# Shared FFN down matmuls in three float32r terms, with split weights and slices

## The reference, cut to what matters

```python
x = x + xattn(layernorm(x), ctx, ...)      # x: 4 x 1024 x 256, ctx: 4 x 77 x 256
# xattn: h = tanh(txt_proj[b,t] + feat_proj[b,f] + bias); rho = h . w; softmax over the 77 rows;
#        the weighted text gives a gate w_s and a shift b_s per token: w_s * x + b_s
# then the FFN on layernorm(x):
probs = softmax(x @ gate)                  # 8 experts
scores, token_idx = top_k(probs.T, k=512)  # each expert takes its 512 best tokens of 4096
h = gelu(tok @ W1 + b1); out_tok = h @ W2 + b2          # 256 -> 1024 -> 256, per expert
routed = scatter_add(out_tok * scores)
shared = gelu(x @ Ws1 + bs1) @ Ws2 + bs2   # 4096 tokens x 256 -> 1024 -> 256
x = x + routed + shared
```

## Time and profile before

| what | us |
| --- | --- |
| median of three runs (898.47 to 903.25) | 899.86 |
| the profiled execution | 903.03 |
| its span, first to last instruction | 901.3 |
| mean granted TensorE clock, share of full speed | 0.982 |
| tanh of block 0 begins / of block 156 begins | 22.0 / 619.1 |
| first up matmul of an expert begins | 696.0 |

### The profile page before, as it was taken

How to read it: one execution, slowest core, us unless ns; L and a number is a source line. 1 busy time by engine, 2 the same in 40 slices (tenths; PEclk the granted TensorE clock), 3 DMA queues, 4 the chain that set the end, 5 groups by cost and what they waited for, 6 DMA issues and landing times.

```text
span 901.3 us, 14092 instructions
## 1 busy us (share of the span) xinstructions
PE 802.9 (89%) x5355; PEld 471.8 (52%) x5355; DVE 710.3 (79%) x1412; ACT 767.6 (85%) x600; POOL 314.0 (35%) x563
## 2 busy tenths in 40 slices
PE   6875579669997999999999999999889999999995
PEld 4321113114442444445354455545766999999985
DVE  4799889897989689988879995884887877667640
ACT  2999999999999999999999999997752676766771
POOL 3310640525444007774002740061303145554423
PEclk8899999999999999999999999999999999999998
DMA  8000000000001000200000010003102365554512
GB/s 263 19 1 1 1 1 1 1 24 1 24 1 47 1 1 1 94 1 1 24 1 1 24 48 1 24 1 117 48 24 77 106 170 140 141 127 108 137 20 34
DMA packets 32405, 41.80 MB, mean 46 GB/s; under 512 B 2365, under 2 KB 29011, under 8 KB 32339
## 3 DMA queue, kind: packets, MB, share of 16 engines
q1 hardware_dynamic: 26083, 32.49, 10.8%
q0 software_dynamic: 6144, 8.39, 5.6%
q10 hardware_dynamic: 112, 0.04, 0.0%
HBM read 28.33 MB, written 12.58 MB: 45 GB/s over the span
## 4 chain that ended last, share of the span: by engine, by line
PE 42%; ACT 37%; issue 10%; DVE 8%; POOL 2%; DMA 1%; ACTq 0%; DVEq 0%; POOLq 0%
ACT z L971 31%; PE bank L890 10%; PE bank L913 9%; PE bank L770 8%; PE bank L821 5%; DVE z L1329 3%; PE bank L806 3%; ACT z L967 2%; ACT u L1008 2%; PE bank L746 1%; PE bank L699 1%; PE bank L928 1%; PE bank L864 1%; DMA vec_rows<-in_L_xattn_w_dram 1%; ACT L1008 1%
## 5 line engine op out<-in xcount | busy, mean ns | idle before, releaser
L971 ACT ACTIVATE z<-z 128x4096 f32<-128x4096 f32 (+5 forms) x157 | 520.7, 3362 | 6.8 <-DVE z L1329 6.6
L1329 DVE TENSOR_SCALAR z<-feat,txt_bias 128x1024 f32<-128x1024 f32 (+1 forms) x722 | 421.2, 657 | 34.8 <-PE bank L770 33.6
L770 PE MATMUL bank<-z,window 128*32 128x512 f32 x2464 | 307.3, 609 | 62.9 <-ACT z L971 61.4
L770 PEld LDWEIGHTS bank<-z,window 128*32 128x32 f32 x2464 | 70.3, 110 | 252.5 <-issue 136.8
L821 PE MATMUL bank<-ws_sb,u 128*128 128x256 f32 x512 | 128.2, 391 | 5.5 <-ACT u L1008 5.5
L821 PEld LDWEIGHTS bank<-ws_sb,u 128*128 128x128 f32 x512 | 93.3, 192 | 41.5 <-issue 19.8
L806 PE MATMUL bank<-tr,ws_s 128*128 128x512 f32 x384 | 107.5, 416 | 0.0
L890 PE MATMUL bank<-xg_s,w_s 128*128 128x512 f32 x384 | 99.6, 397 | 0.2 <-DVE xg_s L1631 0.2
L913 PEld LDWEIGHTS bank<-w_s,hid_s 128*128 128x128 f32 x672 | 86.4, 188 | 4.0
L913 PE MATMUL bank<-w_s,hid_s 128*128 128x256 f32 x672 | 88.2, 280 | 0.0
L1044 ACT ACTIVATE hid<-bank,vec 128x512 f32<-128x512 f32 x64 | 44.2, 690 | 49.4 <-PE bank L890 49.3
(11 more groups left out here) (237 smaller groups left out, 785.6 us busy)
## 6 DMA issues: line engine op xcount, KB each, us to landing
...
x_ring<-in_x_dram SPq DMA_DIRECT2D x8, 512.0 KB, 7.9
xn_dram<-xn SPq DMA_DIRECT2D x8, 512.0 KB, 2.9
out_dram<-x_ring SPq DMA_DIRECT2D x8, 512.0 KB, 2.9
...
xg<-xn_dram,idx POOLq DMA_INDIRECT x32, 3.6
out_dram<-y,idx POOLq DMA_INDIRECT x32, 3.8
```

What stands on the lines that cost most here:

```text
L770: ins = e.matmul(sums[v][32 * r:32 * r + 32, :], window[:, c, 31 - k:63 - k], z[:, n % ZB, at_piece:at_piece + TOK], start=(v, r) not in b ...
L971: e.activation(part, part, ACT.Tanh).then_inc(signal(*step), 1)
L1329: ins = e.tensor_scalar(z[:, n % ZB, i * width:(i + 1) * width], feat_of(units, c), bias_of(units, t, c), None, ALU.add)
```

## The change

The down matmuls take both factors as rounded part and rest, in float32r, and add up three products: rest x part, part x rest, part x part (SPLIT_TERMS). For this

- Ws2 is split at the start in four steps `split_ws2` (part and rest for each half) on GpSimd, at slots 10, 12, 14 and 16 of batch 0; the raw weights are loaded into the u ring's space.
- each gelu slice gets `u_hi`, a rounding copy, on VectorE (for units 0 to 5; `u_hi_last` on GpSimd for 6 and 7), and `u_lo`, slice minus part, on GpSimd. The ring u holds both, so it is twice as large. Gelu writes where the rest goes later.
- FFN_PLACES grows to five stages: up one slot before, gelu one after, u_hi two, u_lo three, down six after (before: up, gelu, down at -1, 1, 2). FFN and the TAIL and PRE places move, and so do the fills behind the loop. Unit 7's downs stand two slices behind its ups instead of one. Of unit 5, the down steps of slices 5, 6 and 7 now come behind the loop (before: slice 7).
- SBUF is laid out anew: one xn2 buffer instead of two, tables of the start and of the router over others' space. This brings waits: `y_norm` of a unit waits for the turn and the store of the unit before; `values` waits for an early tanh; `pick` is cleared by GpSimd behind the loop (`pick_clear`) and no longer at the start. Expert 1 no longer waits for the stored outputs of units 6 and 7 before it rounds its w2.

```diff
@@ -33,30 +33,30 @@
-FFN_STEPS = ("up", "gelu", "down", "down_end", "store_out", "load_x")
+FFN_STEPS = ("up", "gelu", "u_hi", "u_lo", "down", "down_end", "store_out", "load_x")
...
-PRE_EARLY = (17, 19, 20, 22, 23, 23, 27, 24, 28, 29, 30)
-PRE_LATE = (25, 27, 28, 31, 32, 32, 34, 34, 36, 35, 39)
-TAIL_EARLY = (0, 0, 1, 4, 5, 5, 5, 4, 11, 6, 10, 12, 12, 14)
-TAIL_FIRST = (0, 0, 1, 3, 3, 4, 6, 6, 9, 6, 11, 11, 11, 13)
-TAIL_LATE = (0, 1, 2, 3, 8, 9, 10, 9, 13, 11, 15, 16, 16, 24)
-TAIL_SINGLE = (-1, 0, 1, 2, 3, 5, 5, 9, 12, 10, 11, 10, 11, 13)
...
-FFN_PLACES = (-1, 1, 2)
-FFN = ((8, 2.2), (34, 2.1), (13, 2.3), (36, 2.0), (13, 1.5), (26, 1.6))
+PRE_EARLY = (17, 19, 21, 22, 23, 24, 26, 25, 29, 30, 31)
+PRE_LATE = (22, 27, 28, 31, 32, 32, 32, 34, 35, 35, 39)
+TAIL_EARLY = (0, -1, 1, 3, 4, 4, 4, 3, 11, 6, 10, 11, 12, 15)
+TAIL_FIRST = (0, 0, 1, 3, 4, 4, 6, 6, 9, 6, 10, 11, 11, 13)
+TAIL_LATE = (0, 1, 2, 3, 8, 10, 10, 9, 15, 14, 17, 18, 19, 25)
+TAIL_SINGLE = (0, 0, 1, 2, 3, 5, 5, 8, 10, 10, 11, 10, 11, 12)
...
+FFN_PLACES = (-1, 1, 2, 3, 6)
+FFN = ((8, 2.1), (36, 2.0), (13, 3.1), (36, 2.0), (13, 1.8), (26, 1.6))
...
-TAIL_FILL = (8, 4)
-GELUS_BEFORE = 1
+TAIL_FILL = (5, 5)
+GELUS_BEFORE, RESTS_BEFORE = 1, 2
...
-TEST_FILL = (4, 4, 6, 5, 2, 5, 5, 5, 2, 1)
-RANK_FILL = (4, 3, 4, 4)
-EXPERT_FILL = (20, 6, 0)
-SECOND_FILL = (9, 2, 1, 5, 11)
-LIST_FILL = (2, 2, 0, 0)
+TEST_FILL = (1, 5, 4, 4, 4, 6, 4, 5, 4, 1)
+RANK_FILL = (4, 3, 4, 3)
+EXPERT_FILL = (24, 8, 3)
+SECOND_FILL = (7, 2, 1, 4, 8)
+LIST_FILL = (3, 2, 1, 0)
...
@@ -154,6 +154,7 @@
+    at_slots(0, (10, 12, 14, 16), [[("split_ws2", i, h)] for h in range(2) for i in range(2)])
...
@@ -174,7 +175,7 @@
-            at_slots(n, FFN_PLACES, [[("up", v, m, 0, passes)], [("gelu", v, m)], [("down", v, m, 0, J)]])
+            at_slots(n, FFN_PLACES, [[("up", v, m, 0, passes)], [("gelu", v, m)], [("u_hi", v, m)], [("u_lo", v, m)], [("down", v, m, 0, J)]])
...
@@ -204,11 +205,17 @@
     def fill(n=1):
...
-            if filler:
-                order.extend(filler.pop(0))
+            for step in filler.pop(0) if filler else []:
+                order.append(step)
+                if step[0] == "gelu":
+                    order.extend((("u_hi_last", *step[1:]), ("u_lo", *step[1:])))
     def up(v, m):
...
+    def rounding(steps):
...
+        return [(name, *step[1:]) for step in steps if step[0] == "gelu" for name in ("u_hi_last", "u_lo")]
...
@@ -219,7 +226,8 @@
-    last_ffn = up(vb, 0) + [piece for m in range(1, M) for piece in up(vb, m) + down(vb, m - 1)] + down(vb, M - 1)
+    last_ffn = up(vb, 0) + up(vb, 1) + [piece for m in range(2, M) for piece in up(vb, m) + down(vb, m - 2)]
+    last_ffn += down(vb, M - 2) + down(vb, M - 1)
...
@@ -239,14 +247,18 @@
+    order += [step for step in lead if step[0] in ("u_hi", "u_lo") and step[1:3] not in late]
+    waiting = {step[1:3] for step in lead if step[0] in ("u_hi", "u_lo")}
+    late |= waiting
...
+    rests = rounding(held)
...
-    order += [*end[7], *end[9], *end[8], ("logits_exp", vb), ("router", vb), ("values", NT - 2 * J, NT)]
+    order += [*end[7], *rests[:2 * RESTS_BEFORE], *end[9], *rests[2 * RESTS_BEFORE:], *end[8], ("logits_exp", vb), ("router", vb), ("values", NT - 2 * J, NT)]
...
@@ -254,7 +266,7 @@
-    order.append(("digits",))
+    order += [("digits",), ("pick_clear",)]
...
@@ -262,11 +274,11 @@
-        order += [("count", k), ("sign_count", k), ("total", k), *held, *(by_scalar.pop(0) if by_scalar else [])]
+        order += [("count", k), ("sign_count", k), ("total", k), *held, *rounding(held), *(by_scalar.pop(0) if by_scalar else [])]
...
-    order += held
+    order += [*held, *rounding(held)]
...
@@ -449,38 +456,43 @@
-        picked = sb("picked", [P, P], F32R)
...
-        pick = sb("pick", [P, NT, 32], BF16)
-        vals = sb("vals", [P, NT, E, V], BF16)
-        iota_slot = gt[:, 0:P]
-        rest = scan[:, 1, :].rearrange("p (t e) -> p t e", e=E)
-        b2_raw = eq[0:B2_ROWS, :]
...
+        feat_at = cursor[0]
...
-        xn2 = sb("xn2", [P, 2, J, D])
+        xn2 = sb("xn2", [P, J, D])
...
+        att_at = cursor[0]
...
+        b2_raw = sb("b2_raw", [B2_ROWS, D], at=att_at)[:]
+        iota_slot = sb("iota_slot", [P, P], at=att_at + 4 * D)[:]
+        vec_rows = sb("vec_rows", [NV, P], at=att_at + 4 * (D + P))
+        assert D + 2 * P <= 2 * J * R
+        tmp_at = cursor[0]
...
+        ws_sb = sb("ws_sb", [P, C, D], at=tmp_at)
+        assert C * D <= 2 * J * R
...
-        ws_sb = sb("ws_sb", [P, C, D])
+        cursor[0] = max(cursor[0], feat_at + 8 * C * WIDTH + 4 * (2 * HC * TOK + 2 * A * D))
...
-        ws2_sb = sb("ws2_sb", [P, M, D])
+        ws2_s = sb("ws2_s", [P, 2, M, D], F32R)
...
-        u = sb("u", [P, UR, TOK])
+        u_at = cursor[0]
+        u = sb("u", [P, UR, 2, TOK], F32R)
+        u_in = sb("u_in", [P, UR, 2, TOK], at=u_at)
...
@@ -493,7 +505,21 @@
+        tested = sb("tested", [P, NH * P])
+        eq = sb("eq", [P, NH * P])
+        gt = sb("gt", [P, NH * P])
+        picked = sb("picked", [P, P], F32R)
+        assert cursor[0] <= feat_at
+        cursor[0] = feat_at
...
+        vals = sb("vals", [P, NT, E, V], BF16)
+        rest = sb("rest", [P, NT, E])
+        scan = sb("scan", [P, 2, NH * P])
+        pick = sb("pick", [P, NT, 32], BF16)
+        assert cursor[0] <= feat_at + 4 * C * WIDTH and B % 2 == 0
+        cursor[0] = feat_at + 4 * C * WIDTH
...
+        assert cursor[0] <= feat_at + 8 * C * WIDTH
...
@@ -514,7 +540,10 @@
-        ws1_raw = u[:, 0:C * H // TOK, :].rearrange("p m s -> p (m s)").rearrange("p (c h) -> p c h", c=C)
+        u_flat = u_in[:].rearrange("p m i s -> p (m i s)")
+        ws1_raw = u_flat[:, 0:C * H].rearrange("p (c h) -> p c h", c=C)
+        ws2_raw = u_flat[:, C * H:C * H + M * D].rearrange("p (m d) -> p m d", m=M)
+        assert C * H + M * D <= 2 * UR * TOK
...
@@ -637,7 +667,7 @@
-            e.dma_start(ws2_sb[:], Ws2.rearrange("(m p) d -> p m d", p=P)).then_inc(loaded["ws2"], 16)
+            e.dma_start(ws2_raw, Ws2.rearrange("(m p) d -> p m d", p=P)).then_inc(loaded["ws2"], 16)
...
@@ -651,7 +681,7 @@
-                                xn2[:, v % 2]).then_inc(xn2_stored[v], 16)
+                                xn2[:]).then_inc(xn2_stored[v], 16)
...
@@ -809,17 +839,19 @@
                 elif kind == "down":
...
-                        e.wait_ge(loaded["ws2"], 16)
+                        for h in range(2):
+                            e.wait_ge(*done("split_ws2", 1, h))
...
-                    e.wait_ge(*done("gelu", v, m))
+                    e.wait_ge(*done("u_lo", v, m))
...
-                        ins = e.matmul(banks[DOWN[j // 2]][:, j % 2 * D:(j % 2 + 1) * D], u[:, m % UR, j * P:(j + 1) * P],
-                                       ws2_sb[:, m, :], start=False, stop=m == M - 1, skip_group_check=True)
+                        for term, (i, k) in enumerate(SPLIT_TERMS):
+                            ins = e.matmul(banks[DOWN[j // 2]][:, j % 2 * D:(j % 2 + 1) * D], u[:, m % UR, i, j * P:(j + 1) * P],
+                                           ws2_s[:, k, m, :], start=False, stop=m == M - 1 and term == 2, skip_group_check=True)
...
@@ -1005,7 +1037,10 @@
-                    e.activation(u[:, m % UR], banks[up_bank(v, m)][:], ACT.Gelu_apprx_tanh,
+                        for h in range(2):
+                            e.wait_ge(*done("split_ws2", 1, h))
...
+                    e.activation(u_in[:, m % UR, 1], banks[up_bank(v, m)][:], ACT.Gelu_apprx_tanh,
...
@@ -1020,8 +1055,6 @@
-                        e.wait_ge(stored[va], 16)
-                        e.wait_ge(stored[vb], 16)
...
@@ -1177,16 +1209,40 @@
                 elif kind == "y_norm":
...
-                    if v > 1:
-                        e.wait_ge(*done("y_turn", v - 2, C - 1))
-                        e.wait_ge(xn2_stored[v - 2], 16)
-                    normalise(x_ring[:, v % XB], xn2[:, v % 2], x_mv[:, v, :, 0], y_ry[:, v % 2]).then_inc(signal(*step), 1)
+                    if v > 0:
+                        e.wait_ge(*done("y_turn", v - 1, 0))
+                        e.wait_ge(*done("y_turn", v - 1, C - 1))
+                        e.wait_ge(xn2_stored[v - 1], 16)
+                    normalise(x_ring[:, v % XB], xn2, x_mv[:, v, :, 0], y_ry[:, v % 2]).then_inc(signal(*step), 1)
                 elif kind == "whole":
...
+                elif kind == "pick_clear":
+                    e.wait_ge(*done("tanh", LAST - 1))
+                    e.memset(pick[:], 0.0).then_inc(signal(*step), 1)
+                elif kind == "split_ws2":
+                    i, h = args
+                    part = slice(h * M // 2, (h + 1) * M // 2)
+                    e.wait_ge(loaded["ws2"], 16)
+                    if i == 0:
+                        e.tensor_copy(ws2_s[:, 0, part], ws2_raw[:, part]).then_inc(signal(*step), 1)
+                    else:
+                        e.wait_ge(*done("split_ws2", 0, h))
```

(18 more changed lines are left out.)

13 lines of the change are left out of this document (4 added, 9 removed).

## The result

The changed kernel takes **947.9 us** (median of four, 947.3 to 949.6) against 899.8: 1.053 times, 95% interval 1.051 to 1.055. It is slower, as forecast, but the forecast was +12 us and it is +48. The profiled execution took 949.58 us, its span is 947.8.

What follows compares the result with a forecast made beforehand. ScalarE was taken to bound the tanh loop, with the router's search and TensorE's experts behind it. Start +6, loop +8 and behind the loop -2 gave +12 us, 912 us against the median; range 896 to 928.

Steps and rivals of the forecast that it cites:

- start +6: At the start, four split_ws2 operations on GpSimd delay VectorE, for which ScalarE waits: +6 us, between 0.6 and 9.
- loop +8: In the tanh loop, u_hi and u_lo exceed VectorE's idle time in some units, so ScalarE waits: +8 us, limits 0 and 48.
- behind the loop -2: Behind the loop, shorter downs and better filled tests against added slices and waits: -2 us, from -6 to +4.
- A slice's cost in the loop: In the loop, each slice costs VectorE 0.41 us for u_hi and 0.9 for u_lo's port hold, 1.3 us together.
- Two more slices ... +2.8: Behind the last rho, unit 5's slices 5 and 6 now stand there too: +2.8 us.
- GpSimd's fill-time operations don't hurt the counts much; VectorE is there on short steps: Behind the loop, GpSimd's operations during the fill were said to hurt the counts little, VectorE being on short steps.
- The +2.6 at gather 0: Unit 7's slices 6 and 7: rounding queues on GpSimd behind gather 0, their downs ahead of the gathered rows' first turn: +2.6 us.
- The layout, nothing: The single xn2 buffer, moved tables, stores and later clears each counted as nothing; up to 3 us if a load is late.
- (a): Rival: the port is cheap; loop 0, start +1, tail -2 to -5, giving 896 to 899 us; chance 0.22.
- (b): Rival: TensorE's saving counts, in the stretch from 619 to 697 us, giving 892 us; chance 0.13.
- (c): Rival: in the loop, u_lo late in GpSimd's queue blocks TensorE, 2 to 3 us in five units, giving 925; chance 0.15.
- (d): Rival: in the tests, less fill lowers TensorE's clock, +1.7 us each time, inside the tail's range; no chance of its own.

Runs made afterwards that it cites:

- run 1: The changed kernel's order and layout with the old arithmetic (float32 downs, no split_ws2, u_hi, u_hi_last or u_lo), against the kernel before: 915.3 us, ratio 1.017.
- experiment 3: The kernel of run 1 without the line putting unit 5's last down behind unit 6's eight half-ups: 909.5 us; the same edit in the changed kernel: 945.6 us.
- small rounding: The changed kernel with all 64 u_lo and 16 u_hi_last over 4 columns a partition, downs reading the rounded slice in all three terms: 917.3 us.
- run 4: The changed kernel with the u_lo of units 0 to 5 over 4 columns instead of 512, downs reading the rounded slice in all three terms: 929.4 us.
- the holds alone: The kernel of run 1 plus 16 GpSimd casts and 16 subtractions into scratch beside the slices of units 6 and 7, no down waiting: 925.9 us.

## Why the prediction was wrong

The forecast was +12 us, in three terms: start +6, loop +8, behind the loop -2. Two of its steps failed. Behind the loop it took GpSimd's new steps and the rewritten order as nearly free (-2, measured +22.7); this is the larger miss. In the loop it took all of VectorE's idle time in the stretches of the slices as usable (+8, measured +18.8). In medians, each step against the one above it:

| kernel | us | step |
|---|---|---|
| before | 899.9 | |
| + new layout | 903.1 | +3.1 |
| + new order, float32 downs | 915.3 | +12.3 |
| + three terms, u_hi, split_ws2, small u_lo | 917.3 | +2.0 |
| + rounding of units 6 and 7 | 929.4 | +12.1 |
| + u_lo in the loop | 947.9 | +18.5 |

- **The start, +6: right.** The tanh of block 20 comes 5.7 us later behind the first tanh than in run 1, and 7.2 later than in the kernel before. The terms were right too: subtractions of 2.36 and 2.60 us for an estimated 2.9, casts of 1.16 and 1.51 for 1.6 to 2.2.
- **A slice's cost in the loop: right and a little high.** u_hi 0.47 us on average (0.42 median) for 0.41, u_lo 1.46 median for 1.5, its cost to VectorE 0.8 us for 0.9 (the adds' sum on the page went from 421.2 to 465.0 us; 4.9 of that is the start's). VectorE was busy 52.6 us longer where 63 were forecast.
- **The loop's sum, +8: the mechanism right, the size wrong.** The step that failed is "its idle time is spare capacity": summed by unit, all of VectorE's idle time in the six stretches (55.8 us) was counted as usable. Over the whole loop, of 72.8 us 33.8 were used. Of the 39.0 left, 15.8 are still waits for a free z buffer, so at other moments than those where time is short, and some 14 are waits for turns, statistics and gates. And u_hi brings idle time of its own (5.9 us), since it waits in the queue for its GELU. So the loop grew by 18.8, and not by 8; 2 to 4 of that are TensorE's wait for u_lo. The new order, taken as nothing in the loop, adds 1 to 3.
- **Behind the loop, -2: wrong, at +22.7** (274.2 to 296.9), in these terms. (i) "Two more slices ... +2.8" counted their matmuls and not who stands behind them: down_end of unit 5 waits at the head of VectorE's queue, ahead of the last `weigh`. Run 1 reaches the turn of the probabilities 9.0 us later behind the last tanh than the kernel before; 5.5 of them go with the one line of experiment 3, and the other 3.5 were not taken apart. (ii) "GpSimd's fill-time operations don't hurt the counts much; VectorE is there on short steps" was true of the counts (0.47 us in both) and wrong by 12.1 us of what it left out: the steps between two counts and those of the ranks (0.49 us became 1.58, 1.22 became 1.97). Tests and ranks are one serial chain in which each wait counts, and that a step is short did not help it. (iii) The saving of 5.4 us on downs was worth 2.5 (284.3 against 286.8 us behind the last tanh, small rounding against run 1). (iv) The -2.5 of the tests' new fill was right, in run 1: 25.2 us against 27.5. With the rounding they take 29.7. The -1 of the ranks did not come. (v) The +2.6 at gather 0 came (14.4 us from the first expert's gather to the second's for 12.1), but only in part by the rounding: run 1, without any, has 14.1, three terms with small rounding 12.9, and the tail's rounding brings it to 14.3.
- **The layout, nothing: wrong by 2 to 3 us**, in the experts, cause open. The places that were looked at (y_norm, the stores, the tables) did hold.
- **Rivals.** (a), the port is cheap, is refuted by the start and run 4. (b) is there, 2.5 us, and buried. (c) was small in this kernel (downs wait 3.6 us for u_lo) and is real: with u_hi and u_lo a slot later it cost 14.8 us. (d), the colder clock, is part of the tests' 29.7 us; the kernels with small rounding and with the holds alone have a clock of 1.00 there, so it comes where holds and downs that wait for rounded slices meet; the two were not taken apart.
- Of what would show it, the adds beside u_lo (1.48 us in the median, for 0.48) and the ScalarE wait at the start (5.57 us) came as written. The saving per slice did at full clock (from the first start to the last end 1.69 us in the median for 1.99), but all slices together saved 10.0 us and not 20. VectorE was over 95% busy in two of five units, ScalarE idle by 1 to 5 us a unit; the last tanh came at 643 instead of 633, and the last section longer by 23 instead of shorter by 2.

On the port itself the rule cited from the Trainium skill (SBUF — State Buffer, "SBUF: two separate sides") agrees with the adds of 7.60 us at the start and of 3.90 us in the loop. As the prediction puts it, it is too wide: that section has VectorE take the shared pair of ports only in a two-port mode or with two inputs in SBUF, and here the counts, of one large input, kept their 0.47 us; which mode the counts and the adds are in, no run tells. The estimate of 1.1 us from the Trainium skill (GPSIMD Engine Reference, "Performance versus the Vector engine") would have made the loop's term less than about 4; the u_lo measured, 1.26 us at the least and 1.46 in the median beside a busy VectorE, is nearer to the drawn-out row's 1.5. Its cost to VectorE was 0.7 us as a hold alone and 0.8 in the changed kernel; by the prediction's working the Trainium skill's figure gives 0.7 and the row 0.9, so the cost alone does not decide between the two.
